# A two-layer decoder: the expert stage as two passes of 39 tiles whose first sums are scattered into the second queue, in place of 85 tiles and gathers

## The reference

```
def _L1_ffn_ref(x, gate_w, gate_b, w1, b1, w2, b2):
    xf = x.reshape(b * t, d)                      # 8192 rows of 256
    scores = xf @ gate_w + gate_b                 # 8 experts
    topk_s, topk_i = jax.lax.top_k(scores, TOP_K) # TOP_K = 2
    comb = jnp.zeros_like(scores).at[jnp.arange(n)[:, None], topk_i].add(topk_s)
    h = jnp.maximum(jnp.einsum('nd,edh->neh', xf, w1) + b1, 0.0)
    eo = jnp.einsum('neh,ehd->ned', h, w2) + b2
    out = jnp.einsum('ne,ned->nd', comb, eo)
...
x = x + _L1_xattn_ref(_layernorm(x, axis=-1), ctx_1024, ...)
x = x + _L1_ffn_ref(_layernorm(x, axis=-1), ...)
```

## Time and profile before

| | us |
|---|---|
| median of 3 runs | 2748.13 |
| lowest, highest | 2747.97, 2748.63 |
| span of the profiled execution | 2732.5 |
| what the median has above that span | 15.6 |

### The profile page before, as it was taken

How to read it: one execution, slowest core, us unless ns; L and a number is a source line. 1 busy time by engine, 2 the same in 40 slices (tenths; PEclk the granted TensorE clock), 3 DMA queues, 4 the chain that set the end, 5 groups by cost and what they waited for, 6 DMA issues and landing times. The chain is left out here.

```text
span 2732.5 us, 49486 instructions
## 1 busy us (share of the span) xinstructions
PE 2354.2 (86%) x16048; PEld 1842.8 (67%) x16048; DVE 1869.3 (68%) x4490; ACT 1643.3 (60%) x3283; POOL 1352.9 (50%) x1313
## 2 busy tenths in 40 slices
PE   5999999669999958999999999986999898599881
PEld 3667676559999835565665656654787777599881
DVE  3888888545656437777777777772777777477783
ACT  3777777545555426776766767663444343388883
POOL 4777777453334255455454545521556565202556
PEclk9999999779999978999999999996999999799996
DMA  2222222152222001111111111113233433355896
GB/s 62 73 67 74 70 71 66 40 168 73 86 65 66 18 29 32 42 39 43 41 41 42 38 42 39 33 39 127 86 117 121 137 124 107 128 160 181 275 279 199
DMA packets 236524, 241.65 MB, mean 88 GB/s; under 512 B 36926, under 2 KB 222528, under 8 KB 236144
## 3 DMA queue, kind: packets, MB, share of 16 engines
q1 hardware_dynamic: 214704, 192.11, 23.0%
q0 software_dynamic: 20480, 46.39, 5.3%
q10 hardware_dynamic: 1088, 0.00, 0.0%
HBM read 132.78 MB, written 101.25 MB: 86 GB/s over the span
## 5 line engine op out<-in xcount | busy, mean ns | idle before, releaser
L1554 DVE TENSOR_REDUCE f_nm<-f_raw 128x4 f32<-128x1024 f32 x256 | 312.8, 1222 | 107.5 <-PE f_raw L1667 104.6
L1390 POOL TENSOR_TENSOR f_hm<-f_hm,f_mhalf 128x64 f32<-128x64 f32 x32 | 366.4, 11449 | 2.7
L1459 ACT ACTIVATE f_PT<-f_sco 128x1024 f32<-128x1024 f32 x256 | 262.2, 1024 | 99.1 <-PE f_sco L1684 98.7
L2399 POOL DMA_INDIRECT d_pick<-expert_out,e_out_slots x128 | 133.2, 1041 | 221.7 <-DMA expert_out<-d_eo 135.7
L916 ACT ACTIVATE b_hT<-b_H,b_b1r 128x512 f32<-128x512 f32 x128 | 88.4, 691 | 162.4 <-PE b_H L1046 147.0
L1684 PE MATMUL f_sco<-f_q4T,f_k4T 64*128 64x256 f32 x1024 | 130.9, 336 | 51.0 <-DMA f_q4T<-f_nmT 36.6
L1925 POOL DMA_INDIRECT expert_in<-g_xm,e_slots x128 | 129.8, 1014 | 40.2 <-issue 37.0
L677 PE MATMUL a_bank<-a_w,a_xnT 128*128 128x512 f32 x256 | 127.1, 621 | 21.9 <-ACT a_xnT L394 21.9
L1061 PE MATMUL b_O<-b_w2l,b_hTh 128*128 128x256 f32 x512 | 145.9, 285 | 0.0
L1061 PE MATMUL b_O<-b_w2h,b_hTh 128*128 128x256 f32 x512 | 144.7, 283 | 0.0
L1061 PE MATMUL b_O<-b_w2h,b_hTl 128*128 128x256 f32 x512 | 143.6, 280 | 0.0
(11 more groups left out here) (368 smaller groups left out, 7722.3 us busy)
## 6 DMA issues: line engine op xcount, KB each, us to landing
e_xs<-expert_in SPq DMA_DIRECT2D x85, 256.0 KB, 3.3
expert_out<-d_eo SPq DMA_DIRECT2D x85, 256.0 KB, 2.5
x_scratch<-a_x SPq DMA_DIRECT2D x64, 256.0 KB, 3.1
b_w<-in_L_ffn_W_dram SPq DMA_DIRECT2D x16, 1024.0 KB, 5.7
a_x<-in_x_dram SPq DMA_DIRECT2D x32, 256.0 KB, 3.8
a_cx<-in_ctx_dram SPq DMA_DIRECT2D x32, 256.0 KB, 3.4
f_x<-x_scratch SPq DMA_DIRECT2D x32, 256.0 KB, 2.7
f_q4T<-f_nmT SPq DMA_DIRECT2D x128, 64.0 KB, 2.3
```

Source lines behind the costliest of these rows:

```text
L1390: g.tensor_tensor(hm[b % 2][:, :], hm[b % 2][:, :], mhalf[:, :], ALU.pow).then_inc(hroot, 1)
L1459: s.activation(PT[n % 3][:, t, :, :], heads(SCO), ACT.Exp, scale=float(DH) ** -0.5).then_inc(probs_ready, 1)
L1554: v.tensor_reduce(nm[:, t, g * HG:(g + 1) * HG], heads(RAW), AX.X, ALU.max, negate=True)\
L2399: g.indirect_dma_start(pick[b % GR][:, t, c, :], None, ex.eo_d[k], bass.IndirectOffsetOnAxis(ap=ex.out_slots[:, b, t, c:c + 1], axis=0), b ...
```

## The change

Filing: a row is filed once with everything that it needs. The first queue's rows are 2·272 values wide (2176 B): x5 with its score and target, and the normalised row with its score and target; the second queue's are 272 wide (1088 B, the normalised row). x5 is no longer stored apart. There is one queue per choice over all 32 sequences (no blocks), so 32 + 7 = 39 tiles for the first choices and 39 for the second, 78 in all. The tile list for the first 17 tiles is made in four slots near the end (`early_table`), the rest in two tables after the last slot (`final_table`, 19 steps each). Padding tiles are written in experts_phase, in its first 32 steps.

Experts: SP loads tile m into one of XR = 8 buffers once the scatters out of that buffer have landed. After `add_b2` DVE computes own + score · z in the same buffer (`finish`, two instructions of 128x256), and POOL scatters the 256 rows with two indirect DMAs: in the first pass to `first_out`, at the row's place in the second queue, in the second pass straight to the output (rows of padding are out of range and skipped). In the second pass SP also loads the first sums (`load_part`), and waits before the first of these until all scatters of the first pass have landed. `finish` runs two tiles late in the first 16 tiles of the second pass, one late in the next 8. The bias copy moves from DVE to ACT. Stores, x5 loads, gathers, weighting and the two additions per sequence are gone. Nothing else of the program changes. The core of the diff:

```diff
-        self.BLOCKS = (B // 2 - 1, B // 4 + 2, B // 4 - 1)
-        self.NE, self.TILE, self.RAW = NE, 2 * P, 6
-        most = max(self.BLOCKS) * S
...
-        self.tiles = [2 * n * S // self.TILE + NE - 1 for n in self.BLOCKS]
...
+        self.W = D + 16
+        self.OUT_OF_RANGE = 1 << 18
+        self.region = B * S + self.TILE
+        self.spare = NE * self.region
+        self.rows = self.spare + self.TILE
+        self.SNAP = 3 * B // 4
+        self.EARLY = self.SNAP * S // self.TILE - (NE - 1)
+        self.TILES = B * S // self.TILE + NE - 1
+        self.WHOLE = (B * S - NE * (self.TILE - 1) + self.TILE - 1) // self.TILE
+        self.queue_d = [nc.dram_tensor("first_in", (self.rows, 2 * self.W), F32).ap(),
+                        nc.dram_tensor("second_in", (self.rows, self.W), F32).ap()]
+        self.part_d = nc.dram_tensor("first_out", (self.rows, D), F32).ap()
...
-        self.XR = 6
-        self.xs = [sb(f"xs{n}", [P, self.TILE // P, D]) for n in range(self.XR)]
+        self.XR, self.WR, self.AHEAD = 8, 4, 4
+        self.xs = [sb(f"xs{n}", [P, T, 2, self.W]) for n in range(self.AHEAD)]
+        self.w1l = [sb(f"w1l{n}", [P, 1, C, D], F32R) for n in range(self.WR)]
...
+    def load_tile(self, sync, m):
+        k = m // self.TILES
+        row = sync.value_load(self.row[0:1, m:m + 1], min_val=0, max_val=self.spare)
+        sync.dma_start(self.xs[m % self.XR][:, :, k:, :], self.queue_d[k][bass.ds(row, self.TILE), :]
+                       .rearrange("(p t) (k w) -> p t k w", p=P, w=self.W)).then_inc(self.xs_loaded[m % self.XR], 16)
...
+            sync.wait_ge(table_step, EARLY_STEPS)
             for r in range(YR):
-                sync.wait_ge(x5_stored[r], 16 * len(range(r, B, YR)))
+                sync.wait_ge(filed[r], 64 * len(range(r, ex.SNAP, YR)))
+            for m in range(ex.AHEAD):
+                ex.load_tile(sync, m)
...
+                g.iota(meta[b % YR][:, :, 1, :], [[P, T], [0, 1]], base=b * S, channel_multiplier=1).then_inc(tok_ready, 1)
+                pool.wait_ge(tok_ready, b + 1)
...
+                        slot = (first_slot[b % YR][:, t:t + 1], meta[b % YR][:, t, 0, :])[k]
+                        row = pk[b % YR][:, t, k:, :].rearrange("p k w -> p (k w)")
+                        g.indirect_dma_start(ex.queue_d[k], bass.IndirectOffsetOnAxis(ap=slot, axis=0), row, None,
+                                             bounds_check=ex.rows - 1, oob_is_err=False).then_inc(filed[b % YR], 16)
...
-                    dve.wait_ge(x5_stored[b % YR], 16 * (b // YR))
+                    dve.wait_ge(filed[b % YR], 64 * (b // YR))
...
+            def early_table(b):
+                if b == ex.SNAP - 1:
+                    whole_tiles(0)
...
+            def final_table(k):
+                whole_tiles(k)
+                made(v.tensor_tensor(ex.pad_row[k][:, :], count[:, :], regions[:, :], ALU.add))
+                if k == 0:
+                    made(v.tensor_tensor(tiles_of[:, 0:NE], whole[:, :], done[:, :], ALU.subtract))
+                    made(v.scalar_tensor_tensor(first_row[:, 0:NE], done[:, :], float(ex.TILE), regions[:, :], ALU.mult, ALU.add))
+                else:
+                    made(v.tensor_copy(tiles_of[:, 0:NE], whole[:, :]))
+                    made(v.tensor_copy(first_row[:, 0:NE], regions[:, :]))
+                made(v.scalar_tensor_tensor(first_row[:, NE:Q], whole[:, :], float(ex.TILE), regions[:, :], ALU.mult, ALU.add))
+                sum_up(Q)
+                at = (ex.EARLY, ex.TILES)[k]
+                n = ex.TILES * (k + 1) - at
+                lay_out_rows(at, n, Q + 1)
+                lay_out_experts(at, n, Q + 1)
...
+            for k in range(2):
+                final_table(k)
...
+    N, HALF, XR, WR, ZR = 2 * ex.TILES, ex.TILES, ex.XR, ex.WR, 4
+    LOADS, PARTS, LAG = 5, 2, 2
...
+        xm = lambda m, t, c: xs[m % XR][:, t, 1, c * P:(c + 1) * P]
+        own = lambda m, t: xs[m % XR][:, t, 0, 0:D]
+        coef = lambda m, t: xs[m % XR][:, t, of_class(m), D:D + 1]
+        target = lambda m, t: xs[m % XR][:, t, of_class(m), D + 1:D + 2].bitcast(I32)
...
                 if m >= XR:
-                    sync.wait_ge(xT_psum, m - XR + 1)
-                ex.load_tile(sync, m, k, j)
-
-            def store(m):
-                k, j = TILES[m]
-                sync.wait_ge(eo_ready, m + 1)
-                sync.dma_start(ex.eo_d[k][j * ex.TILE:(j + 1) * ex.TILE, :].rearrange("(t p) d -> p t d", p=P),
-                               eo[m % ER][:, :, :]).then_inc(eo_stored[m % ER], 16)
-
-            def load_x5(b):
-                if b >= GR:
-                    sync.wait_ge(summed, b - GR + 1)
-                sync.dma_start(x5[b % GR][:, :, :], x5_rows[b]).then_inc(x5_loaded[b % GR], 16)
-
-            def store_out(b):
-                sync.wait_ge(summed, b + 1)
-                sync.dma_start(out_rows[b], y[b % 2][:, :, :]).then_inc(out_stored[b % 2], 16)
-
-            for b in range(GR):
-                load_x5(b)
-            for m in range(N + 1):
-                if m + XR - 1 < N:
-                    load(m + XR - 1)
-                if m < N:
-                    store(m)
-                for b in merged_after(m - 2):
-                    store_out(b)
-                    if b + GR < B:
-                        load_x5(b + GR)
-            for b in merged_after(N - 1) + merged_after(N):
-                store_out(b)
-                if b + GR < B:
-                    load_x5(b + GR)
-            for u in range(2):
-                sync.wait_ge(out_stored[u], 16 * (B // 2))
+                    sync.wait_ge(scattered[m % XR], 16 * T * turn(m))
+                if m % HALF == ex.WHOLE:
+                    sync.wait_ge(pads_filed[of_class(m)], 16 * T * NE * (1, 2)[of_class(m)])
+                ex.load_tile(sync, m)
...
+            def load_part(m):
+                if m == HALF:
+                    for r in range(XR):
+                        sync.wait_ge(scattered[r], 16 * T * len(range(r, HALF, XR)))
+                row = sync.value_load(ex.row[0:1, m:m + 1], min_val=0, max_val=ex.spare)
+                sync.dma_start(xs[m % XR][:, :, 0, 0:D], ex.part_d[bass.ds(row, ex.TILE), :]
+                               .rearrange("(p t) d -> p t d", p=P)).then_inc(part_loaded[m % XR], 16)
+
+            def pad(k, e):
+                row = sync.value_load(ex.pad_row[k][0:1, e:e + 1], min_val=0, max_val=ex.spare)
+                for t in range(T):
+                    sync.dma_start(ex.queue_d[k][bass.ds(row + t * P, P), :].rearrange("p (k w) -> p k w", w=ex.W),
+                                   ex.pad[:, k:, :]).then_inc(pads_filed[k], 16)
+                    if k == 1:
+                        sync.dma_start(ex.part_d[bass.ds(row + t * P, P), :], ex.pad[:, 0, 0:D]).then_inc(pads_filed[k], 16)
+
+            for m in range(ex.AHEAD, LOADS):
+                load(m)
+            for i in range(N):
+                if i + LOADS < N:
+                    load(i + LOADS)
+                if i == HALF:
+                    for m in range(HALF, HALF + PARTS):
+                        load_part(m)
+                if HALF <= i < N - PARTS:
+                    load_part(i + PARTS)
+                if i < 2 * NE and i % 2 == 0:
+                    pad(0, i // 2)
+                if 2 * NE <= i < 4 * NE and i % 2 == 0:
+                    pad(1, i // 2 - NE)
...
+            for m in range(N):
+                pool.wait_ge(finished, m + 1)
+                stand_alone(pool, pool_passed)
+                table = (ex.part_d, out_rows)[of_class(m)]
+                for t in range(T):
+                    g.indirect_dma_start(table, bass.IndirectOffsetOnAxis(ap=target(m, t), axis=0), own(m, t), None,
+                                         bounds_check=table.shape[0] - 1, oob_is_err=False).then_inc(scattered[m % XR], 16)
...
+                e = act.value_load(ex.expert[0:1, m:m + 1], min_val=0, max_val=NE - 1)
                 if m >= 3:
                     act.wait_ge(up_psum, m - 2)
+                    act.wait_ge(relu_ready, C * (m - 2))
+                s.activation(bias[m % 3][:, :, :], b1[:, bass.ds(e, 1), :], ACT.Copy).then_inc(bias_ready, 1)
                 s.activation(w1h[m % 3][:, :, :, :], wh[0][:, bass.ds(e, 1), :, :], ACT.Copy).then_inc(w1_high, 1)
...
+                e = held[m] = dve.value_load(ex.expert[0:1, m:m + 1], min_val=0, max_val=NE - 1)
+                if m >= WR:
+                    dve.wait_ge(up_psum, m - WR + 1)
+                v.tensor_copy(w1l[m % WR][:, :, :, :], wl[0][:, bass.ds(e, 1), :, :]).then_inc(w1_low, 1)
...
+            def finish(m):
+                dve.wait_ge(z_ready, m + 1)
+                if of_class(m):
+                    dve.wait_ge(part_loaded[m % XR], 16 * part_turn(m))
+                for t in range(T):
+                    last = v.scalar_tensor_tensor(own(m, t), z[m % ZR][:, t, :], coef(m, t), own(m, t), ALU.mult, ALU.add)
```

(14 more changed lines are left out.)

## The result

The kernel after takes 2716.44 us (median of 4 runs, 2711.27 to 2719.97), the kernel before beside it 2748.05 (2747.77 to 2748.63); the ratio is 0.9886, 95% interval [0.9867, 0.9904]. That is 31.6 us off, 1.1%, where 65 were predicted: the sign and the range held, the size was forecast at twice its value.

What follows compares the result with a forecast made beforehand. PE was taken to bound the expert stage at 3.30 us per tile, with waits for the ring of eight buffers. The terms summed to −64.9 us, a span of 2667.6; with 15.6 added, 2683 us, range 2648 to 2724.

Steps and rivals of the forecast that it cites:

- cross_pass: tables, constants, its end: cross_pass: two tables out of the slots −17.9, constants at the start +1.4, two tables after the last slot +2.5 us.
- seven tiles and the old stalls: Experts: seven fewer tiles at 3.30 us, −23.1 us, and the stalls of the kernel before gone, −16.6 us.
- first pass: Experts, first choices: 3.42 us per tile by the ring, 3.6 by the DMA engines; +9.8 us (0 to 20).
- turn of the passes, 6 tiles: Between the passes: load 45, queued behind the wait for all first-pass scatters, lands 14.2 us after tile 38's `down`; +4.3 us.
- two late, 14 tiles: Second pass, finish two tiles late: the ring gives 4.83 us per tile for 14 tiles, +21.4 us.
- one late, 8 tiles: Second pass, finish one tile late: the ring gives 3.63 us per tile for 8 tiles, +2.6 us.
- tail: From the last `down` to the end: 8 us in place of 57.3, −49.3 us.
- DVE and POOL: Experts, per tile: DVE 3.15 us, 0.15 under PE's 3.30; POOL's two scatters about 2.6 us, hidden.
- Rival 3: Experts: POOL's indirect DMAs keep DVE out, 5.15 us per tile, +110 us, 2793 us in all; chance 0.05.
- F: Experts: time from the end of `down` to the next load's landing in that buffer; 13.8 us first pass, 11.2 second.
- a rival with a lower clock: Second pass: a lower granted clock, ending at the same place as rival 2, 2716 us; within its chance of 0.20.
- Rival 2: Experts: DMA saturates and PE slows; second pass +24 us, first pass +9 us, 2716 us in all; chance 0.20.

Runs made afterwards that it cites:

- base: The kernel after, unchanged, timed a second time against the kernel before: 2728.87 us, ratio 0.9921.
- xr12: The kernel after with twelve buffers in place of eight, late finishes kept at the same tiles: 2684.85 us, ratio 0.9757.
- repeat1: xr12 with the first pass done again as the second: wide loads, first targets, no part loads, late finish or padding: 2658.58 us, ratio 0.9673.
- wideout: repeat1 with the second targets and scores, its indirect DMAs going to the output: 2658.61 us, ratio 0.9677.
- contigt: xr12 with a partition's two rows adjacent in the second pass, tile loads eight ahead, part loads four, fewer late finishes: 2674.58 us, ratio 0.9719.
- plain2: xr12 with POOL issuing plain DMAs to fixed output rows in place of indirect ones in the second pass: 2663.54 us, ratio 0.9676.

## Why the prediction was off, step by step

| term | predicted | measured |
|---|---|---|
| cross_pass: tables, constants, its end | −14.0 | −12.8 |
| seven tiles and the old stalls | −39.7 | −40.5 |
| z(0) after the first transposes | 0 | +1.6 |
| first pass | +9.8 | +19.7 |
| turn of the passes, 6 tiles | +4.3 | +8.0 |
| two late, 14 tiles | +21.4 | +25.3 |
| one late, 8 tiles | +2.6 | +10.9 |
| last 11 tiles | 0 | +0.1 |
| tail | −49.3 | −44.0 |
| sum | −64.9 | −31.6 |

The measured terms are differences of the two profiles, against 3.30 us per tile where a pass is meant; rounded, they add up to 0.1 less than the sum. They are those of one execution each; in base's profile the first pass is +21.1, the second (turn to last tile) +57.3 in place of +44.3, and its last 11 tiles alone +7.7, with three late releases.

**cross_pass.** Right. The slots of after last 12.6 to 13.8 us, but for one of 15.7 near the end, where before has one of 15.6; the constants end 4.2 us after the start in place of 2.75; the last table ends 470.5 us after the start, where the prediction's numbers give 470.0, and the first transposes follow 2.4 us later in place of 1.6.

**DVE and POOL.** Right on the pace. DVE's shortest step from one `add_b2` to the next is 3.06 us with the finish of the same tile (3.15 predicted) and 2.93 with a late one, the last tiles with less work left out. Rival 3 is refuted in its size: 68 of the 78 copies of the low weights took less than 0.45 us, most of them while a scatter was on POOL. But it is there in a small form. The other ten took 0.47 to 0.70 us, six of them 0.6 or more, which the prediction had named as a sign of being wrong. One of them, and the scatter beside it:

```profile
2488.92 0.70 DVE L2448 CAST e_w1l<-e_w1l 128x512 fp32r x1 [0.19 <-issue]
```

```profile
2488.40 0.97 POOL L2387 DMA_INDIRECT first_out<-d_xs  x1 [1.04 <-DVE d_xs L2467]
```

All ten began 0.5 us or more after the start of a scatter and ended 0.25 us after its end; the 51 copies that began 0.19 to 0.41 us after the start of one took 0.42 or 0.43. In sum the ten cost DVE 1.8 us. In the profile of before ten of 85 copies were long in the same way behind the gathers (0.52 to 0.68 us), which the mean of 468 ns in the earlier trace rows hid. The Trainium skill, "SBUF — State Buffer", Who interferes with whom, would have a copy in a 2-port mode and GpSimd exclude each other for a whole instruction; the rows show it for the copies that begin late in a scatter, and not for the others (in which mode the copy runs no row shows).

**The first pass** is the step that failed by the most, 9.9 us. The prediction took the greater of two limits, 3.42 us by the ring and 3.6 by the DMA engines, and the second was no limit at all: xr12 moves the same bytes at 3.34 us per tile, repeat1 and wideout at a share of 0.88 to 0.89. The ring was the limit and was sized too short. In the chain above `down`'s end to the landing is 8.96 us: to the end of `finish` 1.8, 0.87 until POOL starts (0.3 had been taken), 1.27 for the first scatter, 5.06 for the second from its start. SP's load costs 0.7 and its landing 4.6. That is F = 14.3, not 13.8, and gives 3.52 us per tile.

The measured 3.90 (tiles 5 to 38) ask for 16.2, so the turn in the chain is a quick one. The semaphore updates of the trace give the same pieces for the 31 tiles from 8 on (where updates are missing, the last one counts as the landing). In 14 of these, all from tile 12 on, PE's transposes start within 0.4 us of the landing, so there the ring holds PE. Their mean F is 15.9 us: 2.1 to the end of `finish`, 7.1 to the landing of the scatters, 0.8 until SP turns to the load, 1.1 for SP's instructions, 4.8 for the load. That gives (3.3 + 15.9) / 5 = 3.84 us per tile, so the ring accounts for the pace. Of the 1.6 us over the quick turn 1.2 are SP's queue. Between 2438.3 and 2443.2 us it issues two loads with a padding step between them; the buffer of the second was free at 2440.44, and its load's first instruction starts at 2442.18. I had counted the padding as bytes, never as instructions in front of a load. The last six tiles take 3.83 too: the loads of three of them were still issued beside padding, and tile 37's late release of 2.5 us is among them (xr12, whose PE hardly waits in this pass, has 3.67 there).

The Trainium skill, "DMA: Bandwidth & Descriptors", Anatomy of one DMA, gives its fit for DMAs that GpSimd issues. As an estimate by it a scatter should land in 2.3 us; the row above has 5.06, at a DMA share of 0.87. The prediction also put SP's wide load at 3.3 us by this fit, for which the section does not give it; the row has 4.6. Both together are 4.1 us too low, where the prediction's own prices, 3.4 and 4.9, were 1.4 too low.

**The turn.** 8.0 us in place of 4.3. The wait for load 45 that was predicted is there: the step to tile 42 is 4.0 us too long. Before it the step behind tile 37's late release is 1.8 too long, and behind it the wait for load 47, already the ring's, is 2.0; neither was in the sum.

**Two late.** Right in kind, a sixth short: F is 1.7 + 0.87 + 1.27 + 3.71 + 0.7 + 3.19 = 11.4 us (11.2 predicted). But after F come transposes, `up` and `down`, taken at PE's period of 3.30; out of a pause the same 28 matmuls took 3.9 and 4.3 us, and 4.85 at the lower clock. So a turn is 15.3 to 16.6 us, not 14.5. I had a rival with a lower clock and gave it no share in the forecast's sum, though the slots with gaps of the earlier trace rows had shown it: the second pass has 0.88 to 0.95 from tile 38 to 66. (The bounds of 21 and 43 us for F of 10 and 13 come out at 20 and 40 by the prediction's own formulas.)

**One late.** The formula gave 3.63 us, the profile has 4.66. At its start a scatter lands after 5.46 us, SP turns to six of the ten loads 1.3 to 3.6 us after their buffer is free, and three late releases fall in it, one of 3.7 us; how the 8.3 us divide among these is not shown. Late releases were in no case of mine, as nothing like them is in the profile of before: there `add_b2` is never over 0.6 us behind `down` in 85 tiles unless DVE itself is. What they cost the kernel after beside its ring is open; they decide the second pass once there are twelve buffers.

**The tail.** 12.5 us from the last `down` (12.3 from the last `add_b2`) in place of 8. POOL's timeline at the end:

```profile
2698.01 1.21 POOL L2387 DMA_INDIRECT out_dram<-d_xs  x1 [0.30 <-issue]
2699.53 0.98 POOL L2387 DMA_INDIRECT out_dram<-d_xs  x1 [0.31 <-issue]
2700.81 0.98 POOL L2387 DMA_INDIRECT out_dram<-d_xs  x1 [0.30 <-issue]
2702.09 0.97 POOL L2387 DMA_INDIRECT out_dram<-d_xs  x1 [0.30 <-issue]
```

DVE has finished tile 77 at 2698.8, but POOL is then in the scatters of tile 76 and starts the last two at 2700.8; from the start of the last one, 2702.09, to the end of the span are 7.4 us, the landing among them (2.9 to 5.5 us in the chain of this pass). I had the last tile alone on POOL and the landing at 2.5.

**Rivals.** Rival 2 (2716) has the right number by luck and only in part the right mechanism: longer F, lower clock, but no saturated DMA engines. Its 52 us for the second pass are 8 more than measured, and the tail and other terms that it did not touch made up for them. The median of the filings' landings was the wrong price for the scatters: 2.5 us, from a stage with a DMA share of 0.36, put into a pass at 0.4 to 0.6, where the 3.8 beside it is nearer.

**What was to show it.** The chain has the load and the scatter before the transposes of each third tile, as said; the DMA share of the first pass is 0.87 between 2400 and 2450 us and 0.77 on the whole, and it decides nothing; the second pass's windows are 5.1 us per tile, not 4.8; one slot is over 14 us, as in before; six copies of the low weights took 0.6 us or more, with the pace still PE's and the ring's; the tail is not 8.

## What to carry over

A ring of buffers that is freed by a landed DMA must be sized by the landing under the stage's own load, not by the median of a quieter stage; count every instruction of the issuing queue that stands between the freed buffer and its load, and PE's slower restart after each wait. Before blaming bandwidth for a share near 0.9, give the ring more buffers: here four more took 44 us off with the same bytes. And what is deferred to save a wait (the late finish) holds its buffer for as many tiles more: without it the second pass was 12 to 25 us shorter.

## What the runs showed of the hardware

PE's signals can come late while its matmuls go on. In the tile shown above, the trace's semaphore updates have PE's own for `down` at 2506.50 and for the transposes at 2506.56, 2.1 and 1.8 us after the last matmul of each; those of DVE and ACT are on time (2504.30; 2504.36, 2505.03). The one of the `up` that PE does next comes at 2506.68, 0.5 us after its last matmul, about as in the tile before, so PE did go on. Those of landing DMAs stop with PE's: none between 2505.56 and 2506.50, and 16 in the half microsecond after that. The delay is often 2.0 to 2.5 us (six of the nine in xr12's second pass; two more are 4.6 and 4.8); over all runs DVE waits up to 5.9 us (contigt).

An indirect DMA of 128 rows of 1 KB is issued in 0.97 us and lands 2.9 to 5.5 us after its start in the chain of the kernel after; a plain one takes POOL 0.54 us (plain2). In the turns of that chain POOL starts 0.87 us after DVE's `finish` has ended.

The granted clock falls to its lower level (1.2 GHz) in stretches where PE waits long: in xr12's second pass six times, 27 us in all, in wideout's never, in the expert stage of before never between 2376 and 2679 us. The first pass of the kernel after, with PE busy for 131 of 145 us, kept 1.00 too.
